# An attention and feed-forward kernel whose feed-forward part gets a longer prelude before its first slot

## The reference

```python
q = (x   @ Wq + bq) -> 16 heads;  k = (ctx @ Wk + bk) -> 16 heads;  v = (ctx @ Wv + bv) -> 16 heads
scores = q @ k^T / sqrt(32), masked to j < i
attn   = softmax(scores), row 0 set to zero
x1  = layer_norm(x + (attn @ v) @ Wo + bo, g1, be1)
out = layer_norm(x1 + relu(x1 @ W1 + b1) @ W2 + b2, g2, be2)
```

## Time and profile before

| | us |
|---|---|
| median of 3 runs | 2559.17 (2557.25 to 2560.42) |
| the profiled execution | 2560.6 |
| its span, first to last instruction | 2558.8 |
| PE busy | 2471.6 (97%) |
| DVE busy | 2104.3 (82%) |
| ACT busy | 1622.3 (63%) |
| POOL busy | 1572.5 (61%) |
| mean granted TensorE clock | 0.992 of full |

### The profile page before, as it was taken

The page is one execution under the profiler, slowest core; times in us unless marked ns, Lnnn a source line. Parts: engine busy times, 40 slices in busy tenths (PEclk is TensorE's granted clock), DMA queues, the critical chain, the costliest instruction groups (busy, mean ns, idle before and its releaser), DMA issues.

```text
span 2558.8 us, 61632 instructions
## 1 busy us (share of the span) xinstructions
PE 2471.6 (97%) x22668; PEld 1807.7 (71%) x22668; DVE 2104.3 (82%) x4505; ACT 1622.3 (63%) x2882; POOL 1572.5 (61%) x1725
## 2 busy tenths in 40 slices
PE   5999999999999999879999999999999999999998
PEld 2555555555555555458888888888888888888887
DVE  7999999999999998798787778777776877777775
ACT  3899999999999999884344444434344444434343
POOL 2688888877777777675555555555555455545553
PEclk9999999999999999899999999999999999999999
DMA  5444444444444443463222232323223232322320
GB/s 165 116 127 124 127 125 125 127 113 117 116 117 115 109 110 82 122 169 89 51 66 61 59 68 51 70 48 70 57 59 68 58 69 51 66 53 60 67 59 25
DMA packets 444351, 225.57 MB, mean 88 GB/s; under 512 B 302481, under 2 KB 388369, under 8 KB 444050
## 3 DMA queue, kind: packets, MB, share of 16 engines
q1 hardware_dynamic: 442450, 220.33, 35.1%
q10 hardware_dynamic: 1600, 1.31, 0.2%
HBM read 112.45 MB, written 58.25 MB: 67 GB/s over the span
## 4 chain that ended last, share of the span: by engine, by line
PE 65%; DVE 11%; POOL 8%; issue 7%; ACT 4%; SPq 3%; DMA 2%; ACTq 0%; POOLq 0%; DVEq 0%
PE h_ps L1712 22%; PE acc L1728 20%; POOL prob_lo L515 7%; PE front L1698 5%; PE lin_ps L960 5%; PE lin_ps L956 4%; PE max_ps L933 3%; PE st_ps L981 3%; ACT probs L610 2%; PE o_ps L999 2%; DVE max_ps L912 1%; SPq L443 1%; SPq L1105 1%; PE st_ps L1012 1%; DVE top_parts L863 1%
## 5 line engine op out<-in xcount | busy, mean ns | idle before, releaser
L515 POOL TENSOR_TENSOR prob_lo<-probs,prob_hi 128x512 f16<-128x512 f32 (+1 forms) x768 | 775.6, 1020 | 272.8 <-ACT prob_hi L604 250.5
L1712 PE MATMUL h_ps<-x_halves,W 128*128 128x256 f16 x6144 | 755.4, 273 | 3.1 <-ACT hf L1484 3.0
L1728 PE MATMUL acc<-W,hs 128*128 128x256 f16 x5376 | 670.1, 273 | 1.5 <-DVE hs L1666 1.5
L1712 PEld LDWEIGHTS h_ps<-x_halves,W 128*128 128x128 f16 x6144 | 601.0, 98 | 87.4 <-DVE W L1670 2.4
L1484 ACT ACTIVATE hf<-h_ps,b1s,scale_evac 128x256 f32<-128x256 f32 x512 | 284.9, 562 | 539.6 <-PE h_ps L1712 533.3
L1728 PEld LDWEIGHTS acc<-W,hs 128*128 128x128 f16 x5376 | 526.1, 98 | 63.5 <-DVE hs L1666 1.4
L1409 POOL TENSOR_TENSOR hf<-hf 128x256 f32<-128x256 f32 x256 | 246.5, 963 | 470.0 <-ACT hf L1484 469.6
L610 ACT ACTIVATE probs<-st_ps,exp_scale 128x512 f32<-128x512 f32 (+1 forms) x768 | 468.8, 610 | 37.9 <-PE st_ps L1012 33.7
L912 DVE CUSTOM_DVE_ANT_0 max_ps<-max_ps,mask_q 128x256 f32<-128x256 f32 (+2 forms) x768 | 418.4, 567 | 27.2 <-PE max_ps L933 25.2
L604 ACT ACTIVATE prob_hi<-probs 128x512 f16<-128x512 f32 (+1 forms) x768 | 427.8, 557 | 18.2 <-PE o_ps L1001 3.8
L1473 ACT ACTIVATE hs<-hf 128x896 f16<-128x896 f32 x256 | 242.0, 945 | 251.6 <-POOL hf L1412 247.9
(11 more groups left out here) (163 smaller groups left out, 3379.7 us busy)
## 6 DMA issues: line engine op xcount, KB each, us to landing
heads<-stage SPq DMA_DIRECT2D x748, 64.0 KB, 2.0
ctx_rows<-octx SPq DMA_DIRECT2D x64, 264.0 KB, 3.1
o_in<-ctx_rows SPq DMA_DIRECT2D x256, 66.0 KB, 2.7
raw_c<-in_cT SPq DMA_DIRECT2D x64, 256.0 KB, 3.1
raw_x<-in_xT SPq DMA_DIRECT2D x64, 256.0 KB, 3.0
x_in<-in_x SPq DMA_DIRECT2D x32, 512.0 KB, 4.0
x_rows<-x SPq DMA_DIRECT2D x64, 256.0 KB, 2.1
o_in<-x_rows SPq DMA_DIRECT2D x256, 64.0 KB, 2.4
```

The costliest lines, as they stand in the source:

```text
L515: pool.tensor_tensor(prob_lo[:, k % 4, 0:w], probs[:, k % PROBS, 0:w], prob_hi[:, k % 4, 0:w], ALU.subtract).then_inc(pl_done, 1)
L1712: last = pe.matmul(h_ps[:, f % 2, 0:T], W1[:, aw, j, f * P:(f + 1) * P], x1_halves[:, item.parity, aa, j, :], start=(j == 0 and m == 0), s ...
L1728: last = pe.matmul(acc_products[:, n, :], hs[:, p % HS, aa, n, :], W2[:, p, aw, n, :], start=(p == 0 and m == 0 and n % 2 == 0), stop=(p = ...
```

## The change

Only the place of some instructions in the order of each engine is changed, and two places in SP's order. `FEED_AFTER` goes from 46 to 34 and the prelude from 4 to 10 steps, so the feed's slot 0 still follows slot 823. The four `Wo` splits now follow slots 803, 805, 807 and 809. Into the added steps go the work of item 0: `share(0)` after slot 809, the turning of block 0 after 811, its two halves and `share(1)` after 813, the turning of block 1 after 815, its two halves after 817, the spreading of `bv` after 819. `load_second` goes from slot 815 to slot 806; `load_first` stays at 801. SP's first loads of W1 stay after slot 815. A wait of VectorE on the value product of the item before the last (`v_read`) goes from the feed's slot 2 to its slot 6.

```diff
-    FIRST_LOADS = LIN + 4 * UNITS.index(("v", QT - 1)) + 5 - SLOTS
-    SECOND_LOADS = FIRST_LOADS + 14
+    FIRST_LOADS = 33
+    SECOND_LOADS = 38
...
+    PRELUDE = 10
+    TURN_FIRST = KT
...
-        for n in range(KT):
-            if n == 0:
+        for step in range(PRELUDE):
+            if step == PRELUDE - KT:
                 for n in range(FIRST):
                     sp.dma_start(raw_slot(n), chunks[n][0]).then_inc(raw_loaded[n], 16)
             yield
...
     def scalar(act):
-        for j in range(KT):
-            act.wait_ge(bounds.wo_loaded, 16 * KT)
-            act.wait_ge(bounds.ready, 2)
-            act.activation(Wo[:, 0, j, :], early.wo_raw[:, j, :], ACT.Copy, scale=scale_wo).then_inc(wo_hi, 1)
+        for step in range(PRELUDE):
+            if step < KT:
+                act.wait_ge(bounds.wo_loaded, 16 * KT)
+                act.wait_ge(bounds.ready, 2)
+                act.activation(Wo[:, 0, step, :], early.wo_raw[:, step, :], ACT.Copy, scale=scale_wo).then_inc(wo_hi, 1)
+            for u in range(U):
+                if step == TURN_FIRST + 2 * u + 1:
+                    act.wait_ge(ctx_turned, u + 1)
+                    if u == 0:
+                        act.wait_ge(*before.splits_done)
+                    act.activation(turned[:, 0, 0, :, u * P:(u + 1) * P], block_turned[:, :, :], ACT.Copy
+                                   ).then_inc(turned_hi, 1)
+            if step == TURN_FIRST + 4:
+                act.wait_ge(early.columns_loaded, 32)
+                act.activation(bv_wide[:, :, :], bvc[:, :].unsqueeze(2).to_broadcast([P, KT, P]), ACT.Copy
+                               ).then_inc(bv_spread, 1)
             yield
...
     def vector(dve):
+        for step in range(PRELUDE):
+            if step < KT:
+                dve.wait_ge(wo_hi, step + 1)
+                dve.scalar_tensor_tensor(out=Wo[:, 1, step, :], in0=early.wo_raw[:, step, :], scalar=scale_wo,
+                                         in1=Wo[:, 0, step, :], op0=ALU.mult, op1=ALU.subtract).then_inc(wo_lo, 1)
+            for u in range(U):
+                if step == TURN_FIRST + 2 * u - 1:
+                    share(Item(0), u)
+                if step == TURN_FIRST + 2 * u:
+                    turn_context(Item(0), u)
+                if step == TURN_FIRST + 2 * u + 1:
+                    halve_context(Item(0), u)
             yield
...
-                if (window, s) == (0, OTR):
-                    dve.wait_ge(*before.v_read)
...
                         if item.n == 0 and u == 0:
                             dve.wait_ge(values_scaled, 1)
+                            dve.wait_ge(*before.v_read)
...
-FEED_AFTER = 46
+FEED_AFTER = 34
```

More of the change, by code:

```diff
@@ L1382, in gpsimd @@
     def gpsimd(pool):
-        for _ in range(KT):
+        for _ in range(PRELUDE):
             yield
@@ L1432, in scalar @@
                             both = turned[:, item.parity, :, :, u * P:(u + 1) * P]
+                            if kind == 0 and item.n == 0:
+                                continue
                             if kind:
@@ L1488, in vector, with share, turn_context, halve_context @@
     def vector(dve):
[L1489 to L1492, removed]
+        def share(item, u):
+            wait_for(dve, early.o_loaded[u], 64, item, 64)
+            wait_for(dve, ctx_shared, U, item, u + 1 - U)
+            dve.reciprocal(shares[:, u, :], o_in[:, u, :].rearrange("p (h f) -> p h f", f=33)[:, :, 32]
+                           ).then_inc(shares_ready, 1)
+            wait_for(dve, shares_ready, U, item, u + 1)
+            by_head = o_in[:, u, :].rearrange("p (h f) -> p h f", f=33)[:, :, 0:32]
+            dve.tensor_tensor(by_head, by_head, shares[:, u, :].unsqueeze(2).to_broadcast([P, D // 32, 32]),
+                              ALU.mult).then_inc(ctx_shared, 1)
+        def turn_context(item, u):
+            wait_for(dve, ctx_shared, U, item, u + 1)
+            blocks_in = o_in[:, u, :].rearrange("p (k a f) -> p k a f", k=KT, f=33)[:, :, :, 0:32]
+            wait_for(dve, turned_lo, 2 * U, item, u)
+            dve.transpose(block_turned[:, :, :].rearrange("p k (a f) -> p k a f", f=32).bitcast(U32),
+                          blocks_in.bitcast(U32)).then_inc(ctx_turned, 1)
+        def halve_context(item, u):
+            wait_for(dve, turned_hi, 2 * U, item, u + 1)
+            both = turned[:, item.parity, :, :, u * P:(u + 1) * P]
+            dve.tensor_tensor(both[:, 1, :, :], block_turned[:, :, :], both[:, 0, :, :], ALU.subtract
+                              ).then_inc(turned_lo, 1)
+        for step in range(PRELUDE):
[10 more added lines that the diff above has]
+                    halve_context(Item(0), u)
             yield
@@ new lines, in vector @@
+                for u in range(U):
+                    for item, _ in after_first(due(window, s, SLOTS, CHUNKS, OTR + 2 * u + 1)):
+                        halve_context(item, u)
+                    for item in turn_items(window, s, 1, X1_TURN + u):
+                        wait_for(dve, turned_hi, 2 * U, item, U + u + 1)
+                        both = x1_halves[:, item.parity, :, :, u * P:(u + 1) * P]
+                        dve.scalar_tensor_tensor(out=both[:, 1, :, :], in0=block_turned[:, :, :],
+                                                 scalar=scale_x1, in1=both[:, 0, :, :], op0=ALU.mult,
+                                                 op1=ALU.subtract).then_inc(turned_lo, 1)
```

53 lines of the change are left out of this document (11 added, 42 removed).

## The result

The changed kernel takes 2562.23 us (median of 20 runs, 2559.27 to 2566.72) beside 2558.62 us before (20 runs, 2556.23 to 2562.48): a ratio of 1.0015, 95% interval 1.0009 to 1.0022. By the ratio that is 3.8 us slower with an interval of 2.3 to 5.6 us (the medians alone are 3.6 apart): real, and less than the 0.2% named in the prediction. The profiled execution has a span of 2559.4 us, only 0.6 above that of before. So two single profiles hide the difference, and the place where it arises must be found by counting slots.

The account below looks back on a forecast made before the run. ScalarE, as full as TensorE in slots 803 to 815, bounds 816 to 823; then TensorE is full to 1077 us. Terms +1.6 - 0.5 = +1.1 us on a 2559.17 us median gave 2560.3 us, range 2558 to 2563.

Parts of the forecast that it names:

- the first rival: Slots 803 to 815: TensorE is the real bound and hides all added work; 2556.8 us, chance 0.19.
- the second rival: Slots 810 to 815: TensorE waits for ScalarE, stands through slot 809's hole, clock falls to half; 2564.4 us, chance 0.15.
- TensorE's full row behind slot 824 hands on what comes to it: From the first filling matmul to 1077 us TensorE has no hole, so the 1.6 us delay passes on in full.
- ScalarE's high halves up to slot 815: Slots 803 to 815: three more Wo splits of 0.61 us, 1.83 us, less 0.33 us of wait: +1.5 us.
- The first block's high half: Moved to behind slot 813 on ScalarE, it costs its own duration there: +0.52 us.
- The granted clock: Half clock from about 1047 until past 1057 us, price about 1.1 us, left as it was.
- VectorE: Up to slot 815 its added work barely fits; delay of TensorE's next maxima taken as 0, bounds 0 and +2.0 us.
- Slots 816 to 823: ScalarE is the bound: -1.83 for Wo, +1.04 for the second block's high half and bv's spread, -0.8 us.
- The 2.40 us hole can't hide any of it: Slot 809: ScalarE's DMA hole hides none of the added splits, since ScalarE takes its work in order.
- Behind it: After 1077 us: VectorE's second low half is gone, so its second residual comes sooner, worth -0.5 us.
- SP's queue: load_second at slot 806 puts 3.7 us ahead of the heads DMAs; hidden, with 2 us of cover left.

Follow-up runs that it names:

- wo_high_only: Kernel before, with only ScalarE's high halves of Wo moved to behind slots 803 to 809, VectorE's low halves left behind 815 to 821; ratio 1.0007.
- lo_late: Changed kernel, with only VectorE's low halves of Wo put back behind slots 815 to 821; ratio 1.0007.
- turn_only: Changed kernel, with Wo's splits on ScalarE and VectorE kept behind slots 815 to 821; ratio 1.0007.
- wo_only: Kernel before, with only the four Wo splits (both halves) moved to behind slots 803 to 809; ratio 1.0010.
- second_loads: Kernel before, with only load_second moved from slot 815 to slot 806; ratio 0.9998.
- after_no_hole: Changed kernel, with SP issuing all twelve heads DMAs of slot 809, so ScalarE has no DMA hole there; ratio 1.0000.

## Why the prediction was right, and where it was not

The range and the sign held: +1.1 us was forecast, and the interval is +2.3 to +5.6. The size did not, and neither did the mechanism in full. The prediction named what would show it wrong, and two of these signs came. The granted clock was at half in slots 810 to 815. And TensorE had no wait from slot 803's exp to slot 808's and one of 0.30 us before slot 809's, which was to speak for the first rival: up to there the added work did not hold TensorE up; it did at the hole. The exp of slot 816, forecast 2.4 us later, came 4.45 later. That 2562.23 lies inside the forecast's own range of 2558 to 2563 is in part luck: it is about as near to the second rival's 2564.4 as to 2560.3, and that rival, with 0.15, had the part of the mechanism that was missing. What did carry: ScalarE as the full engine ahead of slot 816, and the full row behind slot 824. Step by step:

- **TensorE's full row behind slot 824 hands on what comes to it**: shown. The exps of slots 824 and 834 are both 3.34 us late, and the row is 15.74 us in either kernel.
- **ScalarE's high halves up to slot 815.** Forecast +1.5, and +0.4 for a Wo low half ahead of the `stage` half that the DMAs of slot 809 wait for; wo_high_only, which has all four high halves up to slot 811, shows +1.48 there. The 0.4 was 0.08 (slot 809 at 1.10 in the changed kernel and at 1.02 in wo_high_only): VectorE was nearly through with the Wo half when ScalarE's half of `stage` was done. And the slack was more than the 0.33 us I allowed: four splits of 0.61 are 2.44, of which 0.96 was hidden. By slot 816, where one of the four had stood before, it is +0.87, against 1.9.
- **The first block's high half**: +0.52 forecast, 0.37 from wo_high_only to lo_late and in turn_only.
- **The granted clock** is the term that failed, "I leave it as it was". It fell in the linear layers: lo_late, with the same ScalarE work and no fall, is 3.2 us ahead of the changed kernel at slot 816 and 1.44 at slot 824. These 3.2 us are the fall and TensorE's 1.46 us wait for VectorE together; the runs don't part them. The Trainium skill's rule on the default of half clock (page "TensorE: Matmul & The Clock Gate", Part 1) spoke for this fall, and the trace agrees: the clock went after 0.78 of 2 and 1.34 of 2 us of work, with no stand of more than 1.51 us in between. Two kernels with much the same rows kept the clock, and no run here shows why. I had the place and the mechanism as the second rival with 0.15, at 4.1 us; I took for evidence against it that the same hole had brought no fall before, and did not count that the change leaves TensorE idle 2.06 us around the hole (4.96 less 2.90) where it had been 1.05.
- **VectorE** was put at 0 with a bound of +2.0. TensorE's 1.46 us wait for a maximum is inside that bound. It stands at slot 812 and not, as I had it, at the next group of maxima.
- **Slots 816 to 823**: -0.8 forecast, -0.56 measured up to slot 823 and -1.11 up to 824, since the first fills ran 1.67 us and not 2.30, as the second fall of the clock, at 1057, was short (the clock was up again at 1060.7 us). But the part for Wo alone, -1.83, was wrong: wo_only gives back 0.67 up to slot 823, as one split had been hidden in the hole of slot 819. "The 2.40 us hole can't hide any of it" doesn't hold for that hole.
- **Behind it**, -0.5 was forecast. The second residual does come 0.4 us nearer to the first:

```profile
1083.26 0.75 DVE L1630 SCALAR_TENSOR_TENSOR x<-front,value_scale,x_in 128x512 f32<-128x512 f32 x1 [2.71 <-issue]
...
1087.72 0.75 DVE L1630 SCALAR_TENSOR_TENSOR x<-front,value_scale,x_in 128x512 f32<-128x512 f32 x1 [0.72 <-POOL x_in L1393]
```

The first is 3.35 us late against the earlier trace rows and the second 2.95, each counted from slot 800. But the exps of slots 840 and 848, behind both residuals, are 3.34 and 3.33 late, so nothing of it was handed on to attention; what set those slots was not followed.
- **SP's queue**: hidden, as said; the two kernels without ScalarE's four DMAs show what happens with the cover gone, waits of 1.4 us for `heads`.

What stays open: which of the kernels with Wo's early high halves and the hole lose the clock, as rows that look alike did and did not. Also, the 3.34 us at slot 824 agree with the 3.8 us of the ratio, but in the two profiles the lateness wears off behind slot 848 and is 0.1 us at the end. Counted by VectorE's residuals (L1607 before, L1630 after), of which there are 64, it is 3.35 us at the first, 0.5 at the 17th and 0.04 at the 25th. The profiled execution of before was itself 2 us above the median of its kernel, the other 1 us below, and the other twelve traces change against it from the first to the 25th residual by anything from 3.6 us won to 0.6 lost (second_loads wins 1.4). So that the loss of slots 803 to 824 is the loss of the whole is likely by its size and by after_no_hole's ratio, and not shown by a trace. No version beat the kernel before: second_loads and the two without the hole can't be told from it.

## What to carry to other kernels

Work moved sooner out of a crowded place lands in another: here in slots where ScalarE was as full as TensorE, while the place it left was covered by a row of TensorE work that didn't get shorter. Before such a move, read which engine is full at both ends, and work out on paper what the move does to TensorE's idle time around each hole that is there already: here 1 us more of it came before a fall of the granted clock, and with the wait beside it the price was 3.2 us by slot 816. And count in events, such as one exp a slot, from a common one near by: over some 15 us the shift of each slot was good to some hundredths of a us in single traces, where 20 runs of the whole gave +-1.6 us. Read such a shift at more than one slot, as at a single one two effects can cancel.

## What the runs showed of the hardware

An engine that issues DMAs does not stop at once. ScalarE's four DMAs of slots 809 and 819 appear 26 times in the fourteen traces, and in 23 of them it is 2.66 to 2.71 us from the first DMA to ScalarE's next activation (up to 2.99 in the others). The hole in its work is that time less what it still had in hand as the first DMA started: 1.39 us with 1.31 in hand (before, slot 819), 2.40 with 0.28 (before, slot 809), 2.50 with 0.16 (lo_late, slot 819). And a fall of the clock came without a long stand: TensorE's longest wait before it was 1.51 us.
